# A fused attention, causal top-8 attention and routed feed-forward layer on one core: another order of the step and of the prologue

## The reference

```python
x = x + xattn(layernorm(x), ctx)       # x 64 x 32 x 256, ctx 64 x 257 x 256
x = x + attn(layernorm(x))
x = x + ffn(layernorm(x))

# xattn
Q = x @ Wq + bq;  K = y @ Wk + bk;  V = y @ Wv + bv
K_hat = cos(K @ Wr + br)
out = softmax(Q @ K_hat.T) @ V
# attn: per token the 8 earlier tokens of its sequence most similar to it
A = causal_topk_adjacency(x, 8)
score = where(A < 0.5, -1e9, (x @ W_q.T) @ (x @ W_k.T).T / sqrt(32))
msg = softmax(score) @ x
out = gelu((mix * x + (1 - mix) * msg) * gain + bias) * scale   # mix, scale: two scalars
# ffn: 8 experts, each token goes to the best one
e = argmax(x @ Wr);  p = max(softmax(x @ Wr))
out = p * (gelu(x @ W1[e] + b1[e]) @ W2[e] + b2[e])
```

## Time and profile before

| | |
|---|---|
| time, median of 3 runs | 442.94 us (440.27 to 447.44) |
| the profiled execution | 446.33 us, of which the span from first to last instruction is 444.2 us |
| PE busy | 411.5 us, 93% of the span |
| DVE, ACT, POOL busy | 248.5, 255.9, 237.7 us |
| DMA | 87.46 MB, mean 197 GB/s |
| prologue, to the first scores | 24.56 us |
| steps 1 to 15 | 24.56 to 245.64 us |
| drain and expert blocks | the rest |

### The profile page before, as it was taken

One profiled execution on the slowest core, in us unless ns is written; L12 is line 12 of the kernel. 1 busy time (PEld: TensorE's weight loads), 2 busy tenths in 40 slices (PEclk: granted clock), 3 DMA queues, 4 the chain that ended last, 5 costly groups with the idle time before them and its releaser, 6 DMA issues.

```text
span 444.2 us, 10438 instructions
## 1 busy us (share of the span) xinstructions
PE 411.5 (93%) x3121; PEld 281.9 (63%) x3121; DVE 248.5 (56%) x808; ACT 255.9 (58%) x582; POOL 237.7 (54%) x458
## 2 busy tenths in 40 slices
PE   7977999999999999999898878889999999999991
PEld 7423445454455544545344667679999999998991
DVE  2637478878988888788788655543222222222210
ACT  1474777888888988888678745253333232424240
POOL 1760567767788788888667765451222232222210
PEclk9987999999999999999999998999999999999997
DMA  9897899896986987789999624765685656465100
GB/s 174 188 251 214 216 273 273 202 214 174 278 186 150 240 202 212 185 206 260 190 296 310 220 79 132 234 173 206 239 304 187 200 180 217 165 192 198 57 0 2
DMA packets 119450, 87.46 MB, mean 197 GB/s; under 512 B 78622, under 2 KB 109088, under 8 KB 119268
## 3 DMA queue, kind: packets, MB, share of 16 engines
q1 hardware_dynamic: 111460, 75.96, 62.7%
q0 software_dynamic: 3744, 9.46, 7.0%
q10 hardware_dynamic: 4192, 1.38, 1.7%
HBM read 79.15 MB, written 8.53 MB: 197 GB/s over the span
## 4 chain that ended last, share of the span: by engine, by line
PE 71%; SPq 15%; issue 4%; DMA 4%; DVE 2%; ACT 1%; another core or an unknown queue 1%; POOL 0%; DVEq 0%; ACTq 0%; POOLq 0%
PE pK L1513 19%; PE pT L1500 17%; SPq L575 10%; PE pK L1475 8%; PE pT L1475 7%; PE b L1420 3%; SPq L570 3%; PE b L1659 3%; PE b L1554 3%; PE b L1619 2%; PE b L1598 2%; DMA f_row<-rows_by_token,token_i 2%; DMA token_i<-tokens_by_expert 2%; SPq L563 1%; PE b L1648 1%
## 5 line engine op out<-in xcount | busy, mean ns | idle before, releaser
L1272 ACT ACTIVATE XF<-pT,b_now 128x128 f32<-128x128 f32 x184 | 52.7, 370 | 97.1 <-PE pT L1500 91.8
L1513 PE MATMUL pK<-W,XF 128*128 x368 | 86.6, 387 | 5.9 <-issue 4.1
L1500 PE MATMUL pT<-XF,stage 128*128 128x128 f32 x736 | 87.0, 275 | 0.3 <-issue 0.3
L1500 PEld LDWEIGHTS pT<-XF,stage 128*128 128x128 f32 x736 | 85.9, 192 | 2.1 <-issue 1.1
L1513 PEld LDWEIGHTS pK<-W,XF 128*128 128x128 f32 x368 | 68.8, 193 | 15.5 <-issue 6.9
L409 POOL DMA_INDIRECT f_row<-rows_by_token,token_i x23 | 23.8, 1035 | 83.3 <-DMA out_dram<-XF,token_i 70.3
L1475 PE MATMUL pK<-stage,Wkr 128*128 128x512 f32 x128 | 63.0, 618 | 0.0
L1475 PE MATMUL pT<-stage,Wkr 128*128 128x512 f32 x128 | 61.8, 606 | 1.1 <-DVE stage L726 1.1
L1247 ACT ACTIVATE stage<-stage 128x512 f32<-128x512 f32 x64 | 40.7, 637 | 12.8 <-DVE stage L787 12.6
L787 DVE TENSOR_TENSOR stage<-stage 128x512 f32<-128x512 f32 x64 | 46.2, 722 | 0.7
L726 DVE STREAM_TRANSPOSE stage<-XF 128x1024 f32<-128x1024 f32 x32 | 39.5, 1234 | 12.4 <-DMA XF<-in_ctx_dram 11.3
(11 more groups left out here) (196 smaller groups left out, 666.1 us busy)
## 6 DMA issues: line engine op xcount, KB each, us to landing
stage<-in_L_ffn_W_dram SPq DMA_DIRECT2D x23, 1024.0 KB, 5.4
stage<-in_ctx_dram SPq DMA_DIRECT2D x32, 512.0 KB, 5.4
XF<-in_ctx_dram SPq DMA_DIRECT2D x248, 64.0 KB
W<-in_L_ffn_W_dram SPq DMA_DIRECT2D x8, 1024.0 KB
rows_by_token<-rows_out SPq DMA_DIRECT2D x16, 256.5 KB
ctx_last<-in_ctx_dram SPq DMA_DIRECT2D x64, 32.0 KB, 4.5
X<-in_x_dram SPq DMA_DIRECT2D x1, 1536.0 KB, 7.8
tokens_by_expert<-no_token POOLq DMA_DIRECT2D x2, 576.0 KB, 4.2
```

What stands on the lines that cost most here:

```text
L1272: ins = act.activation(f_hT[b][:, n * P:(n + 1) * P], pT[i][:, (n % 4) * P:(n % 4 + 1) * P], ACT.Gelu, bias=b1_now[:, b, n:n + 1])
L1500: mm = pe.matmul(pT[i][:, (n % 4) * P:(n % 4 + 1) * P], W1[q][:, c, n * P:(n + 1) * P], f_inT[:, q % 2, c * P:(c + 1) * P], start=c == 0, ...
L1513: mm = pe.matmul(p_out, f_hT[q % 2][:, n * P:(n + 1) * P], W2[:, bass.ds(e, 1), n, :].rearrange("p o d -> p (o d)"), start=n == 0, stop=n ...
```

## The change

No instruction of the attention or the experts is added or taken away. In the steps, PE computes unit 0 of the next group's keys (`ctx_project(s + 1, 0, 0)`) near the end of step s in place of at the start of step s + 1; `value_project`, `router` and `message` close the step; DVE transposes half (s + 1, 0) after `fraction(s, 1)`, and does `residual_out`, `route` or `places` ahead of `inverse_sumA`; ACT starts a step with `turn(s, 0)` and `gelu_y`, and its `second_exp` comes after `first_exp`; POOL does `last_value` and `rstd_out` first, and `base`, `last_key` and `mix` last. In step 15 POOL's `rstd_out(11)`, `base`, `last_key` and `mix` now stand ahead of `gather(0)`, and SP's `load_tokens(0)` stands ahead of group 15's row loads. In the prologue the two scalars are loaded by POOL and computed on ACT ahead of its half of `Wkr`; four of the loads of half (1, 0) go from SP to ACT; SP sends the rows of group 0 ahead of half (1, 1), and half (2, 0) ahead of `bv`, `Wv` and group 1's rows.

```diff
--- before.py
+++ after.py
+            for k, name in enumerate(("log_mix", "log_scale")):
+                pool.dma_start(logs[:, k:k + 1], a["L0_attn_" + name].partition_broadcast(P)).then_inc(S["logs_ld"], 16)
...
             for s in range(1, NG):
                 if s >= 2:
                     rstd_h(s - 2)
-                    base(s - 2)
+                if s >= 2:
                     normal_h(s - 2)
-                if s == 3:
-                    own_parts()
-                if s >= 3:
-                    mix(s - 3)
-                last_key(s)
                 last_value(s - 1)
                 if s == 1:
                     pool.wait_ge(S["bv_ld"], 16)
                     add_bv(0)
                     add_bv(1)
-                if s == NG - 1:
-                    scatter(s // 2 - 3)
-                    gather(0)
-                if s == 2:
-                    pool.wait_ge(S["w_ld"], 16 * W_LOADS)
-                if s == NG - 1:
+                if s >= 4:
                     rstd_out(s - 4)
-                if s >= 2:
-                    messages(s - 2)
                 if s >= 6 and s % 2 == 0:
                     count_pair(s // 2 - 3)
                     tokens_of(s // 2 - 3)
-                if s >= 7 and s % 2 and s + 1 < NG:
-                    scatter(s // 2 - 3, (0,))
-                if 4 <= s < NG - 1:
-                    rstd_out(s - 4)
+                if s >= 7 and s % 2:
+                    scatter(s // 2 - 3, (0,) if s + 1 < NG else (0, 1))
+                if s == 2:
+                    pool.wait_ge(S["w_ld"], 16 * W_LOADS)
+                if 2 <= s < NG - 1:
+                    messages(s - 2)
+                if s >= 2:
+                    base(s - 2)
+                last_key(s)
+                if s == 3:
+                    own_parts()
+                if s >= 3:
+                    mix(s - 3)
                 if s + 1 < NG:
                     rstd_x(s + 1)
+                if s + 1 < NG:
                     normal_x(s + 1)
+                if s + 1 < NG:
                     add_bv(s + 1)
                 if s in (2, 3):
                     no_tokens(s - 2)
                 if s >= 7 and s % 2 and s + 1 < NG:
                     scatter(s // 2 - 3, (1,))
+                if s == NG - 1:
+                    gather(0)
+                    messages(s - 2)
...
-            for j in range(2):
-                load_by_feature(1, 0, j)
+            load_by_feature(1, 0, 0)
+            load_ctx(0, 0)
+            load_last(0, 0)
             sp.wait_ge(S["ctxT_r"], 2)
             for j in range(2):
                 load_by_feature(1, 1, j)
-            load_ctx(0, 0)
-            load_last(0, 0)
+            sp.wait_ge(S["ctxT_r"], 3)
+            for j in range(2):
+                load_by_feature(2, 0, j)
             sp.dma_start(bv[:], a["L0_xattn_bv"].partition_broadcast(P)).then_inc(S["bv_ld"], 16)
             sp.dma_start(Wv[:], rows(a["L0_xattn_Wv"])).then_inc(S["w_ld"], 16)
             load_ctx(1, 1)
             load_last(1, 1)
-            sp.wait_ge(S["ctxT_r"], 3)
-            for j in range(2):
-                load_by_feature(2, 0, j)
...
+                if g == NG - 1:
+                    load_tokens(0)
                 next_group(g, g % 2)
...
+            ctx_turned(0, 1)
             whole(0, 0)
             fraction(0, 0)
-            ctx_turned(0, 1)
             next_stats(1)
             whole(0, 1)
             fraction(0, 1)
             next_moments(1)
             last_copy()
-            ctx_turned(1, 0)
+            scalars()
             whole(0, 2)
             fraction(0, 2)
+            ctx_turned(1, 0)
...
             for s in range(1, NG):
                 if s >= 2:
                     residual_stats(s - 2)
-                if s + 1 < NG:
-                    next_stats(s + 1)
                 if s >= 2:
                     residual_moments(s - 2)
                 ctx_turned(s, 1)
+                whole(s, 0)
+                score_max(s - 1)
+                if s >= 4:
+                    residual_out(s - 4)
+                if s >= 6 and s % 2 == 0:
+                    route(s // 2 - 3)
+                if s >= 7 and s % 2:
+                    places(s // 2 - 3)
+                    probability(s // 2 - 3)
+                if s >= 4:
+                    out_stats(s - 4)
+                inverse_sumA(s - 1)
+                if s >= 4:
+                    out_moments(s - 4)
+                if s + 1 < NG:
+                    next_stats(s + 1)
+                fraction(s, 0)
+                whole(s, 1)
                 if s >= 3:
                     inverse_sumB(s - 3)
+                fraction(s, 1)
+                if s + 1 < NG:
+                    ctx_turned(s + 1, 0)
+                if s == NG - 1:
+                    plan_experts(1)
+                mean_value(s - 1)
...
             act.wait_ge(S["consts"], made_at["ident"])
-            act.activation(sumA[:], ident[:, 0:1], ACT.Sin)
+            act.dma_start(Wq[:], rows(a["L0_xattn_Wq"])).then_inc(S["wq_ld"], 16)
+            act.dma_start(bq[:], col(a["L0_xattn_bq"]), allow_slow_non_contiguous=True).then_inc(S["wq_ld"], 16)
+            act.dma_start(Wqk[0:H, :], a["L0_attn_W_q"]).then_inc(S["wqk_ld"], 16)
+            act.dma_start(Wqk[H:2 * H, :], a["L0_attn_W_k"]).then_inc(S["wqk_ld"], 16)
+            act.wait_ge(S["logs_ld"], 2 * 16)
+            act.activation(sc[:, 0:1], logs[:, 0:1], ACT.Exp, scale=-1.0).then_inc(S["scal_act"], 1)
+            act.activation(sc[:, 5:6], logs[:, 1:2], ACT.Abs).then_inc(S["scal_act"], 1)
+            act.wait_ge(S["scal_act"], 2)
+            act.activation(sc[:, 6:7], sc[:, 5:6], ACT.Exp, scale=-1.0).then_inc(S["scal_act"], 1)
+            act.wait_ge(S["scal_act"], 3)
+            act.activation(sc[:, 7:8], sc[:, 6:7], ACT.Ln, bias=1.0).then_inc(S["scal_act"], 1)
             act.wait_ge(S["wkr_mm"], 2)
             act.mul(Wkr[:, 1, :], pT[1][:, 0:D], INV_2PI).then_inc(S["wkr_half"], 1)
-            act.dma_start(bq[:], col(a["L0_xattn_bq"]), allow_slow_non_contiguous=True).then_inc(S["wq_ld"], 16)
-            act.dma_start(Wq[:], rows(a["L0_xattn_Wq"])).then_inc(S["wq_ld"], 16)
-            act.dma_start(Wqk[0:H, :], a["L0_attn_W_q"]).then_inc(S["wqk_ld"], 16)
-            act.dma_start(Wqk[H:2 * H, :], a["L0_attn_W_k"]).then_inc(S["wqk_ld"], 16)
-
-            def scalars():
-                act.wait_ge(S["logs_ld"], 2 * 16)
-                act.activation(sc[:, 0:1], logs[:, 0:1], ACT.Exp, scale=-1.0).then_inc(S["scal_act"], 1)
-                act.activation(sc[:, 5:6], logs[:, 1:2], ACT.Abs).then_inc(S["scal_act"], 1)
-                act.wait_ge(S["scal_act"], 2)
-                act.activation(sc[:, 6:7], sc[:, 5:6], ACT.Exp, scale=-1.0).then_inc(S["scal_act"], 1)
-                act.wait_ge(S["scal_act"], 3)
-                act.activation(sc[:, 7:8], sc[:, 6:7], ACT.Ln, bias=1.0).then_inc(S["scal_act"], 1)
+            act.wait_ge(S["ctxT_r"], 1)
+            for q in range(P // T):
+                act.dma_start(*quarter_by_feature(1, 0, 1, q)).then_inc(by_feature_ld[0], 16)
+            load_table(ACT.Sin, 0)
...
+            ctx_project(1, 0, 0)
 
             for s in range(1, NG):
-                ctx_project(s, 0, 0)
-                if s == 1:
-                    ctx_project(s, 0, 1)
                 scores(s - 1)
+                xn_T(s)
                 if s >= 7 and s % 2:
                     pe.wait_ge(S["logits_r"], s - 4)
                     rank(s // 2 - 3)
-                xn_T(s)
-                if s >= 2:
-                    ctx_project(s, 0, 1)
+                ctx_project(s, 0, 1)
+                ctx_project(s, 1, 0)
                 probs_T(s - 1)
                 if s >= 2:
                     h_T(s - 2)
-                ctx_project(s, 1, 0)
+                ctx_project(s, 1, 1)
+                values(s - 1, max(0, (s - 5) // 2))
                 if s >= 2:
                     similar(s - 2)
-                values(s - 1, max(0, (s - 5) // 2))
                 queries(s)
-                ctx_project(s, 1, 1)
-                if s >= 2:
-                    small_scores(s - 2)
                 value_T(s - 1)
                 if s >= 4:
                     out_T(s - 4, max(0, (s - 5) // 2))
-                if s >= 3:
-                    message(s - 3)
+                if s + 1 < NG:
+                    ctx_project(s + 1, 0, 0)
+                if s >= 2:
+                    small_scores(s - 2)
                 value_project(s - 1)
                 if s >= 4:
                     router(s - 4)
+                if s >= 3:
+                    message(s - 3)
```

88 lines of the change are left out of this document (31 added, 57 removed).

## The result

| | changed kernel | kernel before, same comparison |
|---|---|---|
| median of the runs | 449.49 us (447.61 to 451.75) | 444.52 us (440.27 to 447.44) |
| ratio | 1.0153, 95% interval 1.0109 to 1.0198 | 1 |
| profiled execution | 451.75 us, span 449.7, clock 0.968 | 446.33 us, span 444.2 |

The change made the kernel 1.5% slower: within 2%, and inside the range of 436.5 to 451.5, but 5.7 us above the number I gave and outside the 440 to 448 of the forecast itself. Where the 5.5 us between the two spans lie is read from the places where `scores` and `in_T` start. Windows of the changed kernel, the columns as in the earlier trace rows: step 2's last third, step 7, steps 14 and 15, and 226 to 232 us.

What follows compares the result with a forecast made beforehand. PE's own work was taken to bound steps 3 to 13, leaving only the prologue and stalled steps to win. Terms of -3.7, +1.5, +0.3 and +2.8 gave +0.9 us on 442.94: 443.8 us, range 436.5 to 451.5.

Steps and rivals of the forecast that it cites:

- the forecast itself: Whole kernel: the main case, 440 to 448 us, given a chance of 0.48.
- Term 1: Prologue on ACT: Wkr 2.5 us late, first turn at about 15.5, first scores at 25.5, 0.9 us later.
- Term 2: Prologue on SP: the wait at half (2, 0) goes, step 3's scores start at 56.0, gain 3.7 us (2.2 to 5.2).
- the sign that SP isn't the cap: Prologue: step 3's scores starting earlier than 54 would show that SP's issuing does not cap the gain.
- Term 3: Full steps: the new order keeps PE full with thin slacks, late loads now show; loss 1.5 us (0 to 3).
- the step's chain is too long: Full steps: POOL's normal_x comes late and PE waits at xn_T in 11 steps; 449 to 456 us, chance 0.17.
- Term 4: Step 14: its end is worse placed as DVE's plan moves into step 15; loss 0.3 us (-0.3 to 0.9).
- Term 5: Gather of block 0: starts 13.4 us into step 15, rows land at 18.8; loss 2.8 us (1.0 to 4.4).
- The sum: Whole kernel: -3.7 + 1.5 + 0.3 + 2.8 = +0.9 us, put on the median of 442.94.
- nothing is given back: Steps and block 0: gather lands early or the drain has room, thin slacks hold; 437 to 439 us, chance 0.25.
- The prologue is slower: Prologue: ACT's 3.4 us not won back, lower clock after PE's gap, Term 2 gives 0; 447.5 us, chance 0.10.

Runs made afterwards that it cites:

- a_scal: Changed kernel with the scalars' activations put back on ACT in step 1, behind the weight loads and Wkr; 449.91 us, ratio 1.0162.
- best3: best2 with the edit of a_scal (scalars' activations back on ACT in step 1); 442.86 us, ratio 0.9966 to the kernel before.
- before2: The kernel before, unchanged, profiled a second time; 442.24 us (one), span 440.2 us.
- a_mix: Changed kernel with POOL's base and mix put ahead of last_key and messages in a step; 447.48 us, no ratio given.
- a_tok: Changed kernel with SP's load_tokens(0) put back behind group 15's context rows and W2; 446.25 us, ratio 1.0101.
- b_pro: Kernel before with only the prologue of the change (POOL, SP, DVE, ACT ahead of the loops); 444.04 us, ratio 1.0034.
- a_pg: Changed kernel with plan_rows(0) and plan_used(0) at the end of step 13 and POOL's gather(0) ahead of last_value(14); 445.65 us, ratio 1.0070.
- best2: a_best with SP's loads of W2 moved behind the halves of the next, even group; 444.24 us, ratio 1.0017 to the kernel before.
- a_best: a_pg with the POOL order of a_mix and, in odd steps, the first scatter ahead of last_value; 445.54 us, ratio 1.0103.
- a_gather: Changed kernel with POOL's gather(0) in step 15 put back right behind the scatters, ahead of rstd_out(11), base, last_key and mix; 448.55 us, ratio 1.0133.

## Why the prediction was right or wrong

**Term 1** had the place, and under a third of the size. ACT's `Wkr` came at 12.07 (11.75 was given). The first `turn` came at 16.39, not 15.5, and for another reason. Timeline of ACT:

```profile
8.82 1.28 ACT L1227 ACT_TABLE_LOAD   x1 [8.82 <-issue]
10.12 0.20 ACT L1227 ACTIVATE sc<-logs 128x1 f32<-128x1 f32 x1
...
10.69 1.33 ACTq L1237 DMA_DIRECT2D XF<-in_ctx_dram  x3
...
12.55 1.28 ACT L1212 ACT_TABLE_LOAD   x1
13.85 0.20 ACT L1212 ACTIVATE unread<-ident 128x1 f32<-128x1 f32 x1
16.39 0.69 ACT L1245 ACTIVATE stage<-pK,bkr 128x512 f32<-128x512 f32 x1 [2.34 <-PE pK L1478]
```

ACT was ready at 14.05 and waited for PE: I had put the four context loads in a row with its own work, and they went out beside it. PE was late since the lower clock followed the 2.63 us gap (0.50 from 12.53 to 16.00): 6.66 us for eight matmuls, which took 3.70 before. I had that clock as a rival at 0.10 and it belonged into the term. First scores: +3.2, not +0.9. The Trainium skill (ScalarE: Activation LUTs, What ACT_TABLE_LOAD costs) gives 1283 ns for a table load and some 1380 ns for a drain beside it. The load agrees (1.28). The drain shows in none of these rows: the next activation starts 1.30 us after the load did.

**Term 2** was right that the wait at (2, 0) would go and that loads from SP would hold DVE next. PE at step 3 was 1.96 us early, against 2.2 to 5.2. But the wait did not go to (2, 1), where I looked for it. Timeline of DVE, halves (2, 0), (2, 1), (3, 0), (3, 1):

```profile
32.75 1.24 DVE L729 STREAM_TRANSPOSE stage<-XF 128x1024 f32<-128x1024 f32 x1
42.30 1.25 DVE L729 STREAM_TRANSPOSE stage<-XF 128x1024 f32<-128x1024 f32 x1
51.19 1.25 DVE L729 STREAM_TRANSPOSE stage<-XF 128x1024 f32<-128x1024 f32 x1 [3.87 <-DMA XF<-in_ctx_dram]
60.67 1.25 DVE L729 STREAM_TRANSPOSE stage<-XF 128x1024 f32<-128x1024 f32 x1 [1.62 <-DMA XF<-in_ctx_dram]
```

It moved one group on, to (3, 0), and there repeated the pattern of before: `mean_value` behind the waiting transpose, 2.07 us on PE at 52.86, then a clock of 0.67. The other profiles of the order put step 3 at 52.43 to 57.60. The two lowest, 52.75 in a_scal and 52.43 in best3, are those without the scalars ahead of `Wkr`, and they are under the 54 that I had named as the sign that SP isn't the cap. So ACT's prologue held step 3 as well; behind it SP's loads come next (a wait of 2.80 and 2.14 us for half (3, 1)).

**Term 3** named the right slacks and was sized too low. From step 3's start to step 14's the changed kernel takes 157.17 us, before took 153.49 and before2 153.66: a loss of 3.6, where 1.5 (0 to 3) was given. The slack of 0.4 at `select` was gone (waits of 0.47 to 1.07 at `message`). I had counted `mix` for `normal_x`, but not as what `weights_T` and `select` wait for. PE never waited at `xn_T`, so the rival *the step's chain is too long* gave its number (449 to 456) but not its mechanism; `xn_T` was next in line, as a_mix showed. Late halves cost PE 1.03 and 0.80 us in steps 3 and 4, and I had counted 0.8 for one; from 64 to 226 us the runs of this order show 0.5 to 4.5 us of it. The kernels with the order of before show 0.2 to 2.6 us of the same, at `probs_T`, so my sentence that a late half "now" shows was wrong: (10, 1) was not felt because 1.17 us is inside the cover. One premise failed the other way. I had said that another order can't shorten a full step, but step 5, without a wait and at a clock of 1.00 in both, takes 13.60 us in the changed order and 13.94 before. The waits took more than that gave.

**Term 4**: step 14 took 15.01, 1.0 less than the first profile and 0.8 more than before2's 14.23. With the kernel before itself 1.8 us apart here, +0.3 can't be judged.

**Term 5** is the step that failed. The gather started 13.8 us into the step (13.4 given), the wait ahead of `in_T(0)` was 6.85, and the block came at 21.6, not 18.8. What failed is the sentence "now most loads of the steps are through". I had booked SP's earlier token load as a gain of 1.17 us, and had put the plan at 2.1 us into the same step, without asking what SP does until the plan is there. It stands still, with 4.6 MB of loads and stores behind it. By the traces that cost 4.3 us (a_tok): without it the block comes at 17.3, inside my 17.0 to 20.5.

**The sum** was made at block 0 and is checked there. Measured against the first profile: -2.0 at step 3 (Terms 1 and 2, -3.7 given), +3.7 to step 14 (1.5 given), -1.0 in step 14 (0.3), +5.6 to `in_T(0)` (2.8). That is +6.3 where +0.9 was given. The miss of 5.4 is 2.8 in Term 5, 2.2 in Term 3 and 1.7 in Terms 1 and 2, less 1.3 in Term 4. The drain was to pass it on as it is. It gave back 3.8 us by block 3 (2.2 of them only because the first profile of before was slow there, 39.06 us from `in_T(0)` to `in_T(3)` against 36.82 in before2) and lost 2.0 of it again at block 6, whose rows hang on the last group's routing: `in_T(6)` follows `scores(15)` by 56.1 us in before2, a_tok and the changed kernel alike. I had no term for that chain. After it, behind the wait of 3.82, came 1.6 us of lower clock (5.37 for 32 matmuls, 3.74 in before2), +6.2 at block 7, and the later blocks gave 0.7 back: the end is +5.5. That the time still lies inside 436.5 to 451.5 is owed to the width of that range and in part to step 14's -1.0, a size by which the kernel before differs from itself: the misses of Terms 1, 2, 3 and 5 all go the same way.

The rival *nothing is given back* is out: neither did the gather land early nor did the thin slacks hold. *The prologue is slower* happened as a mechanism (the gap and the clock); what it costs in the total b_pro leaves between nothing and 3 us. What of the 1.5% belongs to which step is known only by the traces: no single edit undone brought the ratio down to 1, and a_pg, best2 and best3 took it down in parts of 0.5 to 0.9% whose intervals overlap. Together the edits are clear of noise: best2 and best3 (at most 1.0058 and 1.0011) lie below the whole interval of the changed kernel (1.0109 to 1.0198). But they also hold moves that before doesn't have (W2, the plan, the early gather).

## What to carry to other kernels

When a load is moved ahead on an issuing queue, look first at what that queue would wait for there: everything behind it is held too, the DMA engines empty, and the backlog then stands in front of whatever is urgent. A list of who waited for an instruction names those that wait for its output, and not those that wait for what stands behind it on its engine: follow the list behind a waiting instruction (here `score_max`, `first_exp`, `probs_T`) and compare the length of the steps, before a wait is called free. And a gain ahead of a chain of latencies (here block 0) is worth only what the next thing asked for (here W1) lets through, so move that too or count nothing.

## What the runs showed of the hardware

PE's clock fell behind gaps of 2.63 us ahead of `Wkr` (0.50 next), 2.07 at `o_norm` (0.67), and 1.25 in a_scal (0.53 from 13.0 to 16.0). The gap of 2.00 us in before2 at block 6 was followed by 1.00, and so was one of 2.72 in a_best, while one of 2.08 in best2 was not (0.76 in its next 2.4 us). The length of the gap alone doesn't tell what follows. Timelines of PE in before2 (the first two rows), a_best and best2:

```profile
300.57 0.44 PE L1420 MATMUL pK<-ident,f_row 128*128 128x128 f32 x2 [2.00 <-DMA f_row<-rows_by_token,token_i]
300.84 3.74 PE L1500 MATMUL pT<-XF,stage 128*128 128x128 f32 x32
...
160.53 1.98 PE L1480 MATMUL pT<-stage,Wkr 128*128 128x512 f32 x4 [2.72 <-DVE stage L732]
...
215.54 2.60 PE L1482 MATMUL pT<-stage,Wkr 128*128 128x512 f32 x4 [2.08 <-DVE stage L734]
```

The same gather of 128 rows took 3.5 us to land in a_tok, 7.7 in the changed kernel and 9.7 in a_gather. SP's stall is not all of it: before took 7.1 without one, and there the megabyte of W1 was asked for at the same moment (238.23, the gather at 238.17), in a_tok 3.8 us ahead of the gather. That what is queued makes the difference is argued from this; no run changes it alone. And ACT's DMA issues ran beside its table load (10.69 and 10.66), at no cost to it.
